# A two-layer conditioned linear-attention block on one core: x and h transposed by DMA instead of TensorE

## The chip, the cores and the metric

The kernel runs on one core of one Trainium2 chip. The metric is the device time in microseconds of one execution. Engines are named TensorE (PE in the rows), VectorE (DVE), ScalarE (ACT), GpSimd (POOL) and SyncE (SP, which here only issues transfers).

## What is computed

x is (8, 512, 512) in float32: 8 batches of 512 tokens with 512 features. Two layers of the same form follow each other, the first with 8 heads, the second with 16:

```python
xn = layernorm(x) * ln_w + ln_b
q, k, v = xn @ Wq + bq, xn @ Wk + bk, xn @ Wv + bv     # masked tokens leave k and v
q = softmax(q by head, over features)
k = softmax(k, over tokens)
att = k^T v by head;  y = q att
scale, shift = split(silu(cond) @ W_emb + b_emb)       # per batch, "film"
h = (layernorm(y) * ln2_w + ln2_b) * (1 + scale) + shift
x = x + silu(h) @ W_out + b_out
```

## The kernel before, in words

A unit is one batch in one layer; there are 16 units, 0 to 7 in layer 0 and 8 to 15 in layer 1. A unit's token array of 512 x 512 is held as four tiles of 128 tokens, or, turned, as four tiles of 128 features. Every matrix product is done in float16 with each float32 operand split in a high and a low part, three products for one: hi x hi, hi x lo, lo x hi (`split_pairs`). So a stage of four tiles has 48 matmuls.

Each engine has its own program, one `step(u, front, back, following)` after the other: front is the unit whose keys, values and queries are made, back is unit u - 1, whose output is finished, following is u + 1, whose x is prepared. The orders are written by hand, and semaphores join them.

- TensorE: K of unit u (features on partitions), YT (16 float32 transposes of unit u - 1's normalised y, L451), V, Q, attention (48 matmuls of 128 columns into `att_ps`), XT (16 transposes of unit u + 1's normalised x, L451), O (the output product of unit u - 1), Y (48 matmuls of 128 columns).
- VectorE: keys masked from PSUM with their maximum (L835), the statistics of x (L798), the gate that finishes h (L881), low halves of the keys (L861), values (L893), queries: bias, maximum and centring (L922, L925, L927) with their low half (L907), sums of q, the residual (L819), y times 1/sum (L956) and its statistics (L960 to L968).
- ACT: y normalised (L1060), exponents of the keys (L1065), their high half (L1073), tanh and the affine of h from PSUM (L1087, L1094), high half of h (L1055), of the values, x normalised (L1038), exponent and high half of q (L1120, L1124), x's affine after the transpose and its high half (L1045, L1050).
- POOL: the power that gives y_rstd (L1166), the output bias added to x (L1185), x_rstd (L1162), low halves of h (L1215), v (L1176), attention (L1180) and x (L1171), the mask of the next unit (L1193, L1201).
- SP: k's high and low half and q's high and low half are transposed by DMA from SBUF to SBUF (`turn`, L331), 128 x 2048 float16 each. Between them go the loads of x, the store of the result and the mask.

Of the kernel before, what the change touches and what calls it, by code (L numbers as in the profile page):

```python
# [29 lines left out]
RMAX = bass.bass_isa.ReduceOp.max  # L41
# [28 lines left out]
def slot(name, i):  # L70

    return 3 if name == "O'" else slot("O", i) if name == "Y" else SLOTS.index((name, i)) % RING


def previous_user(name, i, u):

    place, now = order(u).index((name, i)), u
    while True:
        if place == 0:
            now = now - 1  # L80
            if isinstance(now, int) and now < -1:
                return None
            place = len(order(now))
            continue
        place -= 1
        before, n = order(now)[place]
        if slot(before, n) == slot(name, i):
            return before.rstrip("'"), n, now + OFFSET[before.rstrip("'")] - (before == "O'")


def build(nc, x_d, emb_d, mask0_d, mask1_d, w_d, bias_d, wemb_d, cols_d, ident_d, blocks_d, out_d):
    with ExitStack() as ctx:
# [12 lines left out]
        w_stage = sb("w_stage", [P, C, D], F32)  # L105

        xh_or_h = sb("xh_or_h", [P, T, D], F32)  # L110
# [42 lines left out]
        ones = sb("ones", [P, P], F32)
# [252 lines left out]
        def _(pe):  # L406
# [17 lines left out]
            def nothing(i):  # L424
                pass
# [869 lines left out]
```

## Time and profile before

| | us |
|---|---|
| median of three runs | 895.27 (894.33 to 895.29) |
| the profiled execution | 894.88 |
| its span | 893.1 |
| TensorE busy | 835.5 (94%) |
| VectorE busy | 717.4 (80%) |
| ScalarE busy | 537.0 (60%) |
| GpSimd busy | 382.5 (43%) |
| DMA engines, mean share | 40% |

The span runs from the first to the last instruction on the core. Busy is the time in which an engine had at least one instruction under way; matmuls overlap, and their ends are modelled. The granted clock of TensorE, a share of 2.4 GHz, was 0.98 on the mean.

### The profile page before, as it was taken

The page shows a single profiled execution, that of the slowest core. Times are in us where ns is not written, and L with a number is a line of the kernel's source. Part 1 is how long each engine was busy: PE and PEld are TensorE (multiplying, and loading weights), DVE is VectorE, ACT ScalarE, POOL GpSimd, SP SyncE. Part 2 cuts the span into 40 slices and gives each one's busy share as a digit, 9 for nine tenths or more (in the row PEclk, how much of TensorE's full clock was granted, in tenths as well). Part 3 has the DMA queues.
Part 4 walks back from the last instruction along what each step waited for, and adds up shares of the span by engine and source line. Part 5 has one row for each costly group of instructions (what it writes and reads, how often), then busy time and mean ns, then how long its engine had stood idle before and what let it go on. Part 6 is the DMA issues. An engine that isn't in the chain of part 4 may idle for free.

```text
span 893.1 us, 13959 instructions
## 1 busy us (share of the span) xinstructions
PE 835.5 (94%) x5245; PEld 457.8 (51%) x5245; DVE 717.4 (80%) x1510; ACT 537.0 (60%) x915; POOL 382.5 (43%) x328
## 2 busy tenths in 40 slices
PE   3677999999999999999999999999999999999967
PEld 2225454464555446455555545555454645555444
DVE  5898897898888788887868978687786978687675
ACT  4356384957757595874837467473838567473713
POOL 1053355434545543453554336455534536455402
PEclk9898999999999999999999999999999999999988
DMA  9922335442525434261644325244343324223322
GB/s 322 349 47 48 106 48 108 94 107 50 138 61 143 106 95 108 50 186 61 189 107 95 95 40 110 64 95 107 95 106 81 88 52 110 73 48 95 48 48 94
DMA packets 162419, 90.83 MB, mean 102 GB/s; under 512 B 134672, under 2 KB 134960, under 8 KB 162352
## 3 DMA queue, kind: packets, MB, share of 16 engines
q1 hardware_dynamic: 162352, 89.94, 39.7%
q8 instruction: 41, 0.67, 0.3%
q14 instruction: 26, 0.21, 0.1%
HBM read 39.60 MB, written 16.78 MB: 63 GB/s over the span
## 4 chain that ended last, share of the span: by engine, by line
PE 63%; DVE 14%; ACT 8%; issue 7%; POOL 4%; DMA 3%; SPq 1%; DVEq 0%; POOLq 0%
PE ring L418 53%; PE ring L451 4%; PE att_ps L418 3%; POOL sb_ht_lo L1215 2%; DVE sb_v_or_q L922 2%; DVE sb_q_max L925 2%; ACT sb_k_or_qt L1065 2%; ACT sb_kq_hi L1073 2%; ACT sb_tanh L1087 2%; ACT sb_xh_or_h L1094 1%; POOL sb_v_parts L1176 1%; DVE sb_y_stats L960 1%; DVE sb_kt_or_y L956 1%; DVE sb_w_lo L720 1%; DVE sb_tanh L907 1%
## 5 line engine op out<-in xcount | busy, mean ns | idle before, releaser
L418 PE MATMUL ring<-sb_w_hi,sb_xt_hi 128*128 128x512 f16 x512 | 195.1, 381 | 4.5 <-DVE sb_k_max L835 2.3
L418 PE MATMUL ring<-sb_w_lo,sb_xt_hi 128*128 128x512 f16 x512 | 195.1, 381 | 0.0
L418 PE MATMUL ring<-sb_w_hi,sb_xt_lo 128*128 128x512 f16 x512 | 194.9, 381 | 0.0
L1060 ACT ACTIVATE sb_kt_or_y<-sb_kt_or_y,sb_y_add,sb_y_rstd 128x512 f32<-128x512 f32 x64 | 46.9, 804 | 167.7 <-DVE sb_y_add L968 167.7
L1215 POOL TENSOR_TENSOR sb_ht_lo<-sb_xh_or_h,sb_ht_hi 128x512 f16<-128x512 f32 x60 | 68.4, 1170 | 114.4 <-ACT sb_ht_hi L1055 114.4
L418 PE MATMUL ring<-sb_xt_hi,sb_w_hi 128*128 128x512 f16 x256 | 97.8, 382 | 7.3 <-DVE sb_xt_lo L997 7.3
L418 PE MATMUL ring<-sb_xt_hi,sb_w_lo 128*128 128x512 f16 x256 | 97.8, 382 | 0.0
L418 PE MATMUL ring<-sb_xt_lo,sb_w_hi 128*128 128x512 f16 x256 | 97.8, 382 | 0.0
L418 PE MATMUL ring<-sb_w_hi,sb_ht_hi 128*128 128x512 f16 x240 | 91.0, 379 | 3.9 <-ACT sb_xh_or_h L1045 3.3
L418 PE MATMUL ring<-sb_w_hi,sb_ht_lo 128*128 128x512 f16 x240 | 91.0, 379 | 0.0
L418 PE MATMUL ring<-sb_w_lo,sb_ht_hi 128*128 128x512 f16 x240 | 91.0, 379 | 0.0
L1120 ACT ACTIVATE sb_v_or_q<-sb_v_or_q 128x512 f32<-128x512 f32 x64 | 40.4, 632 | 80.0 <-DVE sb_v_or_q L927 80.0
L418 PEld LDWEIGHTS ring<-sb_w_hi,sb_xt_hi 128*128 128x128 f16 x512 | 50.6, 99 | 65.7 <-issue 4.7
L418 PEld LDWEIGHTS ring<-sb_w_hi,sb_xt_lo 128*128 128x128 f16 x512 | 50.3, 98 | 61.0 <-issue 1.1
L1185 POOL TENSOR_TENSOR sb_x<-sb_x,sb_bias_o 128x512 f32<-128x512 f32 x64 | 80.7, 1290 | 0.0
L1171 POOL TENSOR_TENSOR sb_xt_lo<-sb_xh_or_h,sb_xt_hi 128x512 f16<-128x512 f32 x60 | 67.6, 1158 | 30.6 <-ACT sb_xt_hi L1050 30.6
L418 PEld LDWEIGHTS ring<-sb_w_lo,sb_xt_hi 128*128 128x128 f16 x512 | 50.3, 98 | 58.5 <-issue 1.0
L1176 POOL TENSOR_TENSOR sb_v_parts<-sb_v_or_q,sb_v_parts 128x512 f16<-128x512 f32 x64 | 76.9, 1233 | 7.0 <-ACT sb_v_parts L1106 7.0
L1065 ACT ACTIVATE sb_k_or_qt<-sb_k_or_qt,sb_k_shift 128x512 f32<-128x512 f32 x64 | 45.4, 710 | 47.7 <-DVE sb_k_shift L843 47.7
L1180 POOL TENSOR_TENSOR sb_att_lo<-sb_att,sb_att_hi 128x512 f16<-128x512 f32 x16 | 18.5, 1159 | 120.9 <-ACT sb_att_hi L1126 120.9
L922 DVE SCALAR_TENSOR_TENSOR sb_v_or_q<-ring,sb_scale_down,sb_bias_q 128x512 f32<-128x512 f32 x64 | 47.7, 745 | 22.9 <-POOL sb_v_parts L1176 20.8
L835 DVE CUSTOM_DVE_ANT_0 sb_k_or_qt<-ring,sb_mask_add,sb_scale_down 128x512 f32<-128x512 f32 x64 | 46.5, 745 | 24.2 <-issue 24.2
(186 smaller groups left out, 1757.8 us busy)
## 6 DMA issues: line engine op xcount, KB each, us to landing
out<-sb_x SPq DMA_DIRECT2D x15, 1024.0 KB, 4.9
sb_x<-out SPq DMA_DIRECT2D x8, 1024.0 KB, 5.8
sb_x<-in_x SPq DMA_DIRECT2D x7, 1024.0 KB, 6.3
sb_mask_raw<-in_mask SPq DMA_DIRECT2D x16, 256.0 KB, 5.9
sb_w_stage<-in_L_cond_Wk SPq DMA_DIRECT2D x2, 1024.0 KB, 6.2
sb_w_hi<-in_L_cond_W_emb SPq DMA_DIRECT2D x2, 1024.0 KB, 11.8
sb_w_lo<-in_L_cond_W_emb SPq DMA_DIRECT2D x2, 1024.0 KB, 12.9
sb_wemb<-in_L_cond_film_emb_W SPq DMA_DIRECT2D x2, 1024.0 KB, 6.2
```

Of the source, the lines that this page charges most:

```text
L418: last = nc.tensor.matmul(out, lhs, rhs, start=(n == 0), stop=(n == len(pairs) - 1))
L451: last = nc.tensor.transpose(out[:, j * P:j * P + P], source(i, j), ident[:])
L835: nc.vector.tensor_tensor_reduce(k_or_qt[:, i, :], bank("K", i), mask_add[:], scale_down[:, front, K_:K_ + 1], -3.4e38, ALU.add, ALU.max, ...
L922: nc.vector.scalar_tensor_tensor(out=q[:, t, :], in0=bank("Q", t), scalar=scale_down[:, front, Q_:Q_ + 1], in1=bias_q[front][:], op0=ALU.m ...
L1060: nc.scalar.activation(kt_or_y[:, t, :], kt_or_y[:, t, :], ACT.Identity, bias=y_add[:, t:t + 1], scale=y_rstd[:, t:t + 1]).then_inc(yh_rea ...
L1065: nc.scalar.activation(k_or_qt[:, i, :], k_or_qt[:, i, :], ACT.Exp, bias=k_shift[:, i:i + 1], accum_out=k_sum[:, i:i + 1]).then_inc(k_exp, 1)
L1120: nc.scalar.activation(q[:, t, :], q[:, t, :], ACT.Exp).then_inc(q_exp, 1)
L1171: nc.gpsimd.tensor_tensor(xt_lo[:, c, :], xh_or_h[:, c, :], xt_hi[:, c, :], ALU.subtract).then_inc(xt_lo_ready, 1)
L1176: nc.gpsimd.tensor_tensor(v_lo[:, t, :], v[:, t, :], v_hi[:, t, :], ALU.subtract).then_inc(v_lo_ready, 1)
L1180: nc.gpsimd.tensor_tensor(att_lo[:], att[:], att_hi[:], ALU.subtract).then_inc(att_lo_ready, 1)
L1185: nc.gpsimd.tensor_tensor(xt(unit, t), xt(unit, t), bias_o[layer][:], ALU.add).then_inc(x_biased, 1)
L1215: nc.gpsimd.tensor_tensor(lo[:, c, :], xh_or_h[:, c, :], hi[:, c, :], ALU.subtract).then_inc(ht_lo_ready, 1)
```

## The change

Everything between the products is arranged anew; the products themselves and their number stay.

1. **x by DMA.** ACT normalises x in token order, rounds it to float16 (`tok_hi`), POOL makes the low part (`tok_lo`), and SP transposes both in two halves each (`turn_x`, behind Q of tile 1 and of tile 3). The weight and the bias of the norm are folded into the projection weights (scaled by ln_w per input row) and their biases (a small product of ln_b with the weights, `shift_parts`, `shift_sums`, `fold`). TensorE still turns x of unit 0.
2. **h by DMA.** y stays in token order. VectorE centres it (`centre`: minus the mean, times a row g), applies rstd and a row s (`affine`), ACT takes the tanh, VectorE gates. The rows g and s of each unit come from a table in DRAM (`film_d`), loaded by `load_rows` into all partitions, 512 KB. The high and low part of h are transposed by `turn_h`. TensorE still turns h of the last unit.
3. **Orders.** In VectorE and ACT, h of unit u - 1 and the keys of unit u are interleaved (`keys_beside_h`, `h_beside_keys`). The low half of q goes from VectorE to POOL. On ACT, x of the next unit is normalised before the exponents of q. The statistics of x run two units ahead, behind the sums of q. In units 0 and 15 the queries are made before the values. Low parts of the weights of layer 1 and of W_out are made on POOL.
4. **Start and end.** Five small loads go through ACT's queue. The last unit finishes h tile by tile (`tail`).

The core of the diff; names not shown are as above. Lines of the programs of ACT and VectorE before:

```diff
-        act.wait_ge(y_affine_ready, u)
...
-            nc.scalar.activation(kt_or_y[:, t, :], kt_or_y[:, t, :], ACT.Identity, bias=y_add[:, t:t + 1],
-                                 scale=y_rstd[:, t:t + 1]).then_inc(yh_ready, 1)
...
-        act.wait_ge(k_shift_ready, u + 1)
...
-            nc.scalar.activation(k_or_qt[:, i, :], k_or_qt[:, i, :], ACT.Exp, bias=k_shift[:, i:i + 1],
...
-            turned = nc.scalar.activation(tanh[:, c % 2, :], bank("YT", c), ACT.Tanh, bias=film_now[:, 1, c:c + 1],
...
-            nc.scalar.activation(xh_or_h[:, c, :], bank("YT", c), ACT.Identity, bias=film_now[:, 3, c:c + 1],
-                                 scale=film_now[:, 2, c:c + 1]).then_inc(film_read, 1)
...
-        normalise_x(u + 1, following, u if back is not None else None)
...
-            nc.scalar.activation(q[:, t, :], q[:, t, :], ACT.Exp).then_inc(q_exp, 1)
...
-            nc.scalar.activation(kq_hi[:, t * D:t * D + D], q[:, t, :], ACT.Copy, scale=ONE).then_inc(q_hi_ready, 1)
...
-        nc.scalar.copy(att_hi[:], att[:]).then_inc(att_hi_ready, 1)
...
-        turned_x(u + 1, following)
...
-        def low_q(t):
-            dve.wait_ge(q_hi_ready, 4 * u + t + 1)
-            nc.vector.scalar_tensor_tensor(out=q_lo[:, t * D:t * D + D], in0=q[:, t, :], scalar=ONE,
...
-                low_q(t - 1)
...
-        low_q(T - 1)
```

VectorE now:

```diff
+def centre(unit, t):
+    dve.wait_ge(rows_loaded, 16 * (unit + 1))
+    nc.vector.scalar_tensor_tensor(out=kt_or_y[:, t, :], in0=kt_or_y[:, t, :], scalar=y_mean_var[:, t, 0:1],
+                                   in1=rows_now[:, 0, :], op0=ALU.subtract, op1=ALU.mult).then_inc(y_scaled, 1)
+def affine(unit, t):
+    dve.wait_ge(y_scaled, 4 * unit + t + 1)
+    dve.wait_ge(y_rstd_ready, unit + 1 + (t if unit == LAST else 0))
+    nc.vector.scalar_tensor_tensor(out=kt_or_y[:, t, :], in0=kt_or_y[:, t, :], scalar=y_rstd[:, t:t + 1],
+                                   in1=rows_now[:, 1, :], op0=ALU.mult, op1=ALU.add).then_inc(z_ready, 1)
+def keys_beside_h(u):
+    for t in range(T):
+        centre(u - 1, t)
+    masked_keys(u, 0)
+    affine(u - 1, 0)
+    affine(u - 1, 1)
+    masked_keys(u, 1)
+    gate(u - 1, 0)
+    affine(u - 1, 2)
+    masked_keys(u, 2)
+    gate(u - 1, 1)
+    affine(u - 1, 3)
+    masked_keys(u, 3)
+    key_shift(u)
+    gate(u - 1, 2)
+    gate(u - 1, 3)
+def step(u):
+    keys_beside_h(u)
...
+    values(u, 0)
...
+        x_affine(u + 1)
+    key_sums(u)
+    values(u, 1)
...
+    low_keys(u, 0)
+    low_keys(u, 1)
+    values(u, 2)
+    low_keys(u, 2)
+    low_keys(u, 3)
+    values(u, 3)
...
+        queries(u, t)
+    mask_attention(u)
+    query_sums(u)
...
+        x_statistics(u + 2)
...
+        find_peak(1, PREPARED[1][u - PREP])
...
+        residual(u - 1, t)
+    attended_all(u)
```

ACT, POOL and SP now:

```diff
+def step(u):
+    h_beside_keys(u)
+    high_values(u, (0,))
+    high_keys(u)
+    high_values(u, (1, 2, 3))
...
+        scale_and_split(0, O_)
+        copy_film(1, 0)
...
+    normalise(u + 1, (0, 1))
+    normalise(u + 1, (2, 3))
...
+        high_queries(u, t)
...
+    high_attention(u)
...
+def normalise(unit, tiles):
+    act.wait_ge(x_affine_ready, unit + 1)
+    if unit > 1:
+        act.wait_ge(k_lo_ready, 4 * unit)
+        act.wait_ge(ht_hi_ready, 16 * (unit - 1))
+        act.wait_ge(h_lo_ready, 4 * (unit - 1))
+    for t in tiles:
+        if t >= 2:
+            act.wait_ge(xp_lo_ready, 4 * (unit - 1) + t - 1)
+        nc.scalar.activation(normalised(unit, t), xt(unit, t), ACT.Identity, bias=x_add[:, t:t + 1],
+                             scale=x_rstd[:, t:t + 1]).then_inc(xh_ready, 1)
+    for t in tiles:
+        act.wait_ge(xh_ready, 4 * unit + t + 1)
+        nc.scalar.copy(tok_hi[:, t, :], normalised(unit, t)).then_inc(xp_hi_ready, 1)
...
+    y_power(u - 1)
+    add_bias(u)
+    low_h(u - 1)
+    low_values(u)
...
+    mask_for(u + 1)
+    low_x(u + 1)
+    low_queries(u)
+    low_attention(u)
...
+        x_power(u + 2)
...
+    turn_h(u)
+    turn_k(u)
...
+        load_x(u + 2)
...
+        load_rows(u)
...
+        turn_x(u)
+    turn_q(u)
...
+        sp.wait_ge(x_new, 4 * u)
+        sp.dma_start(out_d[(u - 1) % B].rearrange("(t p) d -> p t d", p=P), xu(u - 1)).then_inc(out_stored, 16)
```

The start: VectorE's order in unit 0, then what TensorE puts between the key tiles and ahead of the values.

```diff
+    find_peak(0, Q_)
+    masked_keys(0, 0)
+    find_scale(0, Q_)
+    split_low(Q_)
...
+    masked_keys(0, 1)
+    find_peak(0, V_)
+    masked_keys(0, 2)
+    find_scale(0, V_)
+    fold(0, K_)
+    masked_keys(0, 3)
+    key_shift(0)
+    split_low(V_)
+    fold(0, Q_)
+    fold(0, V_)
+    queries(0, 0)
+    queries(0, 1)
...
+    queries(0, 2)
+    queries(0, 3)
+    x_statistics(1)
...
+    gather_film(0)
...
+            film_scales(0)
+    y_moments(0, range(T))
+    x_statistics(2)
+    find_peak(0, O_)
...
+    def with_k(i):
+        if i == 0:
+            sum_w(0, Q_)
+            shift_parts(0, V_)
+        elif i == 1:
+            sum_w(0, V_)
+            shift_sums(0, V_)
...
+    project_keys(0, with_k)
...
+    project_tokens("Q", 0, Q_, xt_hi, xt_lo)
...
+    project_tokens("V", 0, V_, xt_hi, xt_lo, between=with_v)
...
+    pe.wait_ge(shift_folded, folded(0, V_))
+    attention(0)
```

The order of instructions shows two places. The first is on VectorE in layer 1, between y of one unit and the keys of the next. `sb_kt_or_y` is y, `ring` the PSUM banks, `sb_spare` a word that makes VectorE wait, `sb_k_or_qt` the masked keys. Before:

```order
L963 BN_AGGR sb_y_mean_var<-sb_y_stats 128x2 x4
L965 TENSOR_SCALAR sb_y_var<-sb_y_mean_var 128x4
L968 SCALAR_TENSOR_TENSOR sb_y_add<-sb_y_mean_var,sb_y_rstd 128x4
L825 COPY sb_film_now<-sb_film 128x16
L663 MEMSET sb_spare 128x1
L835 ISA sb_k_or_qt,sb_k_max<-ring,sb_mask_add,sb_scale_down 128x512
```

Now, in the same place:

```order
L949 TENSOR_SCALAR sb_y_var<-sb_y_mean_var 128x4
L953 SCALAR_TENSOR_TENSOR sb_kt_or_y<-sb_kt_or_y,sb_y_mean_var,sb_rows_now 128x512 x4
L732 MEMSET sb_spare 128x1
L859 ISA sb_k_or_qt,sb_k_max<-ring,sb_mask_add,sb_scale_down 128x512
L859 ISA sb_k_max 128x1
L959 SCALAR_TENSOR_TENSOR sb_kt_or_y<-sb_kt_or_y,sb_y_rstd,sb_rows_now 128x512 x2
L732 MEMSET sb_spare 128x1
L859 ISA sb_k_or_qt,sb_k_max<-ring,sb_mask_add,sb_scale_down 128x512
L859 ISA sb_k_max 128x1
L964 SCALAR_TENSOR_TENSOR sb_kt_or_y<-sb_tanh,sb_kt_or_y 128x512
L959 SCALAR_TENSOR_TENSOR sb_kt_or_y<-sb_kt_or_y,sb_y_rstd,sb_rows_now 128x512
```

Four centrings of y stand ahead of the first key tile now, and affines and a gate (the row that reads `sb_tanh`) between the key tiles. The copy of film and the product that made y_add are gone.

The second place is on ACT in layer 1, from the high half of h (`sb_ht_hi`, seen before) and the values (`sb_v_parts`) to the exponents of q (`sb_v_or_q` onto itself). `sb_kq_hi` is the high half of k or q, `sb_xh_or_h` and, in the change, `sb_k_or_qt` the normalised x, `sb_tok` its float16 parts. Before:

```order
L1055 CAST sb_ht_hi<-sb_xh_or_h 128x512 x4
L1112 CAST sb_v_parts<-sb_v_or_q 128x512 x4
L1038 ACTIVATE sb_xh_or_h<-sb_x,sb_x_add,sb_x_rstd 128x512 x4
L1120 ACTIVATE sb_v_or_q<-sb_v_or_q 128x512
L1124 ACTIVATE sb_kq_hi<-sb_v_or_q 128x512
```

Now:

```order
L1264 CAST sb_v_parts<-sb_v_or_q 128x512
L1237 ACTIVATE sb_kq_hi<-sb_k_or_qt,sb_k_recip 128x512 x4
L1264 CAST sb_v_parts<-sb_v_or_q 128x512 x3
L1221 ACTIVATE sb_k_or_qt<-sb_x,sb_x_add,sb_x_rstd 128x512 x2
L1225 CAST sb_tok<-sb_k_or_qt 128x512 x2
L1221 ACTIVATE sb_k_or_qt<-sb_x,sb_x_add,sb_x_rstd 128x512 x2
L1225 CAST sb_tok<-sb_k_or_qt 128x512 x2
L1268 ACTIVATE sb_v_or_q<-sb_v_or_q,sb_ln_one 128x512
L1273 CAST sb_kq_hi<-sb_v_or_q 128x512
```

The keys' high half moved behind the first cast of the values, and x is normalised in two pairs, each with its casts, ahead of the exponents of q. The second pair writes where the first stood, so it waits for POOL's low parts of it.

## Rows read from the trace of the kernel before

**Rows 1.** The page: busy time, and one POOL group.

```profile
PE 835.5 (94%) x5245; PEld 457.8 (51%) x5245; DVE 717.4 (80%) x1510; ACT 537.0 (60%) x915; POOL 382.5 (43%) x328
...
L1171 POOL TENSOR_TENSOR sb_xt_lo<-sb_xh_or_h,sb_xt_hi 128x512 f16<-128x512 f32 x60 | 67.6, 1158 | 30.6 <-ACT sb_xt_hi L1050 30.6
```

**Rows 2.** Windows: length, busy of PE, PEld, DVE, ACT, POOL, clock, DMA.

```profile
570.49:621.46 50.97, 50.45 (x322) 27.63 (x320) 39.99 (x83) 31.04 (x55) 24.00 (x21) 1.00 0.37 89
```

**Rows 3.** TensorE's timeline: start us, us, engine line op [idle before].

```profile
594.97 2.84 PE L418 MATMUL att_ps<-sb_kt_or_y,sb_v_parts 128*128 128x128 f16 x48
597.65 1.92 PE L451 MATMUL ring<-sb_ident,sb_xh_or_h 128*128 128x128 f32 x16
599.41 0.38 PE L418 MATMUL ring<-sb_w_hi,sb_ht_hi 128*128 128x512 f16 x1
...
610.45 0.22 PE L418 MATMUL ring<-sb_att_hi,sb_k_or_qt 128*128 128x128 f16 x1 [0.52 <-issue]
```

**Rows 4.** The same timeline, SP's queue.

```profile
604.66 2.30 SPq L335 DMA_TRANSPOSE sb_k_or_qt<-sb_tanh  x1
```

**Rows 5.** L335 on SP: issue ns min/median/max, first and last start.

```profile
L335 SPq DMA_TRANSPOSE sb_k_or_qt<-sb_kq_hi x16: 1317/1810/1987, 78.9 to 854.8; - x16
...
DMA to landing us min/median/max: 4.3/4.7/7.6
```

**Rows 6.** POOL's timeline: the power behind y's variance, units 0, 10, 14.

```profile
93.53 1.03 POOL L1166 TENSOR_TENSOR sb_y_rstd<-sb_y_var,sb_minus_half 128x4 f32<-128x4 f32 x1 [6.36 <-DVE sb_y_var L965]
...
616.95 1.04 POOL L1166 TENSOR_TENSOR sb_y_rstd<-sb_y_var,sb_minus_half 128x4 f32<-128x4 f32 x1 [6.02 <-DVE sb_y_var L965]
...
818.15 1.04 POOL L1166 TENSOR_TENSOR sb_y_rstd<-sb_y_var,sb_minus_half 128x4 f32<-128x4 f32 x1 [5.35 <-DVE sb_y_var L965]
```

**Rows 7.** Timeline in unit 0, bias additions beside low keys.

```profile
48.18 1.28 POOL L1185 TENSOR_TENSOR sb_x<-sb_x,sb_bias_o 128x512 f32<-128x512 f32 x1
...
49.42 1.71 POOL L1185 TENSOR_TENSOR sb_x<-sb_x,sb_bias_o 128x512 f32<-128x512 f32 x1
...
50.11 1.57 DVE L861 SCALAR_TENSOR_TENSOR sb_k_or_qt<-sb_k_or_qt,sb_k_recip,sb_kq_hi 128x512 f16<-128x512 f32 x1
...
51.09 1.71 POOL L1185 TENSOR_TENSOR sb_x<-sb_x,sb_bias_o 128x512 f32<-128x512 f32 x1
```

**Rows 8.** VectorE lines over the span: ns min/median/max.

```profile
L861 DVE SCALAR_TENSOR_TENSOR sb_k_or_qt<-sb_k_or_qt,sb_k_recip,sb_kq_hi x64: 744/752/1700, 48.3 to 835.0; 128x512 f16<-128x512 f32 x64
...
L881 DVE SCALAR_TENSOR_TENSOR sb_xh_or_h<-sb_tanh,sb_xh_or_h x64: 681/691/1678, 110.3 to 882.7; 128x512 f32<-128x512 f32 x64
...
L922 DVE SCALAR_TENSOR_TENSOR sb_v_or_q<-ring,sb_scale_down,sb_bias_q x64: 736/745/752, 65.7 to 851.1; 128x512 f32<-128x512 f32 x64
```

**Rows 9.** Timeline: POOL's mask operation beside a low half of q.

```profile
594.71 1.93 POOL L1201 TENSOR_SCALAR sb_mask_add<-sb_mask_raw 128x512 f32<-128x512 int32 x1
...
595.79 0.68 DVE L907 SCALAR_TENSOR_TENSOR sb_tanh<-sb_v_or_q,sb_kq_hi 128x512 f16<-128x512 f32 x1
```

**Rows 10.** Timeline, 611 to 637: y, exponents, casts of h, values.

```profile
611.39 1.29 DVE L956 TENSOR_TENSOR sb_kt_or_y<-ring,sb_q_recip 128x512 f32<-128x512 f32 x2 [0.67 <-PE ring L418]
...
624.88 0.72 ACT L1065 ACTIVATE sb_k_or_qt<-sb_k_or_qt,sb_k_shift 128x512 f32<-128x512 f32 x1 [2.67 <-DVE sb_k_shift L843]
...
635.46 2.19 ACT L1055 CAST sb_ht_hi<-sb_xh_or_h 128x512 f16<-128x512 f32 x4
...
636.23 2.72 DVE L893 SCALAR_TENSOR_TENSOR sb_v_or_q<-ring,sb_scale_down,sb_bias_v 128x512 f32<-128x512 f32 x4
```

**Rows 11.** TensorE's timeline: the first product of unit 0.

```profile
27.86 0.61 PE L418 MATMUL ring<-sb_xt_hi,sb_w_hi 128*128 128x512 f16 x1 [7.35 <-DVE sb_xt_lo L997]
```

**Rows 12.** Windows in unit 0, columns as in rows 2.

```profile
55.00:60.00 5.00, 2.89 (x14) 1.18 (x13) 4.86 (x14) 0.44 (x1) 0.00 (x0) 1.00 0.56 105
60.00:64.00 4.00, 0.50 (x3) 0.00 (x1) 3.93 (x7) 4.00 (x8) 2.52 (x3) 0.82 0.00 0
64.00:70.00 6.00, 5.93 (x17) 2.49 (x18) 3.88 (x11) 4.85 (x8) 4.14 (x4) 0.55 0.00 1
```

More of the change, by code:

```diff
@@ L70, in slot @@
[L70 to L88, printed above, removed]
+K_, V_, Q_, O_ = range(4)
@@ new lines, with bank_of, previous_user @@
+BANKS = {"K": (0, 1, 2, 3), "first": (4, 5, 0, 1), "second": (2, 3, 4, 5), "O": (0, 1, 2, 3), "Y": (4, 5, 2, 3), "last": (0, 1, 4, 5)}
+def bank_of(name, i, unit):
+    if name in "VQ":
+        name = "first" if (name == "V") != (unit in Q_FIRST) else "second"
+    elif name == "O" and unit == LAST:
+        name = "last"
+    return BANKS[name][i]
+PLACES = [place for u in range(UNITS + 1) for place in order(u)]
+def previous_user(place):
+    here = PLACES.index(place)
+    for before in reversed(PLACES[:here]):
+        if bank_of(*before) == bank_of(*place):
+            return before
+    return None
@@ L460, in film_product, with output @@
[L460 to L468 removed]
+            def output(unit, tiles=range(T)):
+                project_tokens("O", unit, O_, ht_hi, ht_lo, tiles)
@@ L497, in sum_ln @@
-            def sum_ln():
-                pe.wait_ge(ln_peak, LAYERS)
-                for layer in range(LAYERS):
-                    last = nc.tensor.matmul(sums[0][:, 8 + layer:9 + layer], ones[:], peak[:, layer, LN:LN + 1], start=True, stop=True)
-                last.then_inc(ln_summed, 1)
+                last.then_inc(film_turned, 1)
             def bound_film(layer):
                 pe.wait_ge(film_peak, layer + 1)
-                nc.tensor.matmul(sums[1][:, FILM:FILM + 1], ones[:], peak[:, layer, FILM:FILM + 1], start=True, stop=True
-                                 ).then_inc(film_bounded, 1)
@@ L522, in attend @@
+            def attend(u, between=lambda t: None):
                 pe.wait_ge(qt_hi_ready, 16 * (u + 1))
@@ new lines, in last_unit @@
+            def last_unit(u):
+                keys_beside_h(u)
+                queries(u, 0)
+                key_sums(u)
+                queries(u, 1)
+                low_keys(u, 0)
+                low_keys(u, 1)
+                queries(u, 2)
+                low_keys(u, 2)
+                low_keys(u, 3)
+                queries(u, 3)
+                for t in range(T):
+                    values(u, t)
+                residual(u - 1, 0)
+                mask_attention(u)
+                query_sums(u)
+                residual(u - 1, 1)
```

1562 lines of the change are left out of this document (848 added, 714 removed).

## The prediction

> **What bounds the kernel now.** I read the page first, then the stage windows, then one unit of layer 1 in order of time. The page says 835.5 us of TensorE in a span of 893.1, 94% [rows 1]. A unit in the middle tells where that comes from: in 50.97 us TensorE has 50.45 us of work at a granted clock of 1.00, and VectorE is next with 39.99 [rows 2]. In the piece of TensorE's timeline the starts give the prices: attention 2.68 us (594.97 to 597.65), XT 1.76, the four output tiles 10.4 (599.41 to 609.93, less the 0.16 by which a matmul's modelled end runs past the next one's start), then a hole of 0.52 and Y [rows 3]. YT costs what XT does, K, V and Q what O does, and Y about what attention does: 4 x 10.4 + 2 x 2.68 + 2 x 1.76 = 50.5 us. The program is bound by TensorE. The hole is small, but the reader should look at what ends it: q's low half is issued for transposing at 604.66 [rows 4] and a transpose lands 4.7 us after its issue in the median [rows 5], at 609.4, just before the output tiles end. So the chain queries, exponent, split, transpose is nearly as long as its cover.
>
> As marks I take the start of the power on POOL that turns y's variance into y_rstd: 93.53 for unit 0, 818.15 for unit 14, 51.76 us a unit [rows 6]. Thus 93.5 us of start, 724.6 for 14 units, 75.0 of tail. The profiled execution took 894.88 us, 1.8 more than its span and 0.4 under the median of the three runs shown.
>
> **What the change does to each engine in a unit.**
> TensorE loses 32 transposes, 3.5 us, and needs 46.9 us. If it stayed the bound, the 14 units would give back about 49 us.
> ACT loses 12 tile operations: normalising y, the affine of x, and the affine of h. It had 31 us in a unit and is no bound.
> VectorE gains the centring and the affine of y, 8 tile operations. It gives q's low half to POOL, 4. Net 4 x 0.7 = 2.8 us on 40 [rows 2], still under 46.9.
> POOL gains q's low half, 4 subtractions at 1.16 [rows 1], on 24.0 us.
> SP issues 10 transposes instead of 4. Four of the ten are half as large, so it is the work of eight: at 1.8 us for a high half and 2.3 for a low one [rows 4, 5], SP goes from 8 us to 16, plus one load of 512 KB. That is room enough, but SP takes them in order: q waits behind x.
> By busy time the change wins. The loop from one y to the next decides otherwise.
>
> **VectorE against POOL.** In unit 0, the only place where they met, low keys (two operands in SBUF) ran at 1.57 us beside POOL's bias additions, and POOL's additions rose from 1.28 to 1.71 us; the pairs are 1.67 us apart [rows 7]. The same VectorE operation takes 0.75 in the median (1.70 at most), and in the last unit the gate took 1.68 at most against 0.69 [rows 8]. So an operation with two SBUF operands waits for the POOL addition in front of it, and the next addition for it. Operations that read PSUM do not: the bias of q has 752 ns at most [rows 8]. The Trainium skill (SBUF — State Buffer, "SBUF: two separate sides") says that the port pair is an exclusive lock held for the whole instruction, against any GpSimd operation that reads SBUF. By that rule the one-input mask operation would hold VectorE too; here a low part of q beside it kept its 0.68 us [rows 9], so I charge additions and subtractions only. Neither reading changes the sum, since what meets the mask is off the loop.
> The old order keeps the two apart (POOL adds the bias while VectorE reads keys from PSUM). The new one puts four centrings and two affines beside the same additions, and gates and low keys beside POOL's subtractions.
>
> **The loop of one unit in layer 1**, from y's variance (0). A VectorE tile operation follows the last by 0.67 us, an ACT cast by 0.55, an exponent by 0.72 [rows 10].
> 1. Two centrings, 1.34; two more and two affines each in a pair with an addition, 4 x 1.67 = 6.7: 8.0. The first key tile hides in there.
> 2. Seven more (keys, gates, affines) 4.7; one gate behind a subtraction 0.45; the key shift with its waits 0.75: 13.9. Before, keys went first, 7.8 us after the variance: exponents began at 624.88 against 616.95 [rows 6, 10].
> 3. ACT: four exponents at 0.72 with two casts of h between, and the handover: 4.2, 18.1.
> 4. Key sums 0.4. Three value tiles at 0.67 and four low keys at 0.86, 5.45, with one to two waits behind POOL, 0.8 to 1.8: 24.7 to 25.7.
> 5. The last value: cast 0.65; POOL subtraction 1.15, mask 1.95, and two subtractions of x 2.3. ACT can normalise x's last tile only then (two buffers): 0.75 and two casts 1.1. Together 7.9, 32.6 to 33.6.
> 6. ACT's four exponents and casts of q wait behind these in its queue: 4 x 1.33, 37.9 to 38.9.
> 7. SP: high half 1.85, low half landed 4.8 after: 44.6 to 45.6.
> 8. Y's first tile and handover 0.8, then four products, four statistics and moments 5.5 (611.39 to 616.9 [rows 10]): **51.0 to 52.0, taken as 51.5**.
> TensorE's 46.9 us fit inside, so it waits about 4.7 us a unit, some before attention (low keys land at 29 at the earliest) and some before Y.
>
> Layer 0 adds the mask to each value tile and a copy on POOL: 1.5, 53. Units 3 to 6 also have a weight peak (2.3 us and 0.5) between x's statistics and the residual; it leaves 1.8 on the loop, 54.8. Unit 1 has the split of the output weight on ACT before x: eight operations and a copy, 6 us, 59. Low weights now on POOL, folds and the scales stand beside waits and cost nothing; if the loop fell to TensorE's 46.9, they would cost up to 1 us each.
> Sum of 14: 59 + 2 x 53 + 4 x 54.8 + 7 x 51.5 = 744.7, against 724.6: **+20.1**.
>
> **Start.** The first K matmul is at 27.86 [rows 11]. The bound of ln is gone and x needs no affine, so it can start near 21. But then TensorE stands: the key tiles wait for V's peak (VectorE, behind Q's peak and split), the queries for a fold behind V's split. I reach attention 1 us later than before, and then VectorE has the film products, x's statistics for two units and a weight peak (3.1 and 2.8 us) before the first centring, at 101. Bounds: 93 (TensorE's early start kept) and 108. Taken **+7.5**.
>
> **Tail.** Queries first takes q's transpose (4.7 to land) out of the last unit's path; the values come last. By the same prices their low parts are ready 36.7 after the variance of unit 14; attention 2.7, mask, two splits and Y's first tile 3.4: 42.8. Then h is finished tile by tile: 23 VectorE tile operations at 0.67 and four sets of moments at 0.6 to the last gate, 60.6; transpose, cast and low part 2.2, 12 matmuls 2.6, residual 0.8, store 2.3: 68.5 against 75.0, **-6.5** (bounds -12 and +2).
>
> Sum: 894.9 + 20.1 + 7.5 - 6.5 = **916 us**, 2.3% slower.
>
> **Rivals.**
> A, faster. The pairs in steps 1, 2 and 4 do not form, or the loop overlaps more than I let it. Without any lock the loop is 51.5 - 4.0 - 0.45 - 0.8 = 46.2 and TensorE bounds: 47 in layer 1, 49 to 51 in layer 0, with start and tail as above 850; with half of it 882. It decides at 1.5 us a unit: under 50.0 in layer 1 the kernel is faster. For it: all busy times [rows 2]; ACT and SP have room. Against it: the pairs in rows 7. Chance 0.33.
> B, much slower: the clock. TensorE's granted clock fell towards half (1.2 GHz of 2.4) after a hole of 3.5 us at 60 and not after one of 2.1 at 55: the windows show 2.9 us of TensorE in 5 at 1.00, then 0.5 in 4, then 0.55 of the clock [rows 12]. My hole before Y is 2.7 us. If it drops each unit, Y itself doubles, +2.7 on the loop, x14 = 38: 954. Chance 0.12.
> C, level: loop and start errors cancel within 0.2%. Chance 0.04.
> The forecast has the rest, 0.51, with 895 to 940 as its own range.
>
> **The numbers.** About 0.2% is what a measurement of this kernel can tell from no change. Faster is A, 0.33; same C, 0.04; slower the rest, 0.63. The range 862 to 948 leaves out A's best end and B's worst: loop 47.6 to 54, start and tail at their bounds.
>
> **What would show it.** Right: POOL's powers 51 to 52 us apart in layer 1; centrings and the first affines at 1.6 us beside the bias additions; TensorE idle about 2 us before attention and 2 to 3 before Y, ended by the q transpose; exponents of q queued behind x's casts. Wrong: powers under 50 us apart, TensorE without holes, centrings at 0.75; or a granted clock of half in the middle of the program.

## The result

The changed kernel takes 982.65 us, median of four runs (980.25 to 983.43), against 894.8 for the kernel before (893.96 to 895.29): a ratio of 1.098, 95% interval 1.096 to 1.100. The direction was right; the forecast of 916 and its range, which ended at 948, were not. One execution of the kernel with the fourteen extra products below took 1021.9 us at a mean granted clock of 0.83, which was at 0.81 already in the 590 us before the first of these products, and is left out where times are compared.

The page of the changed kernel, its busy line, TensorE's clock in 40 slices and the start of the chain that ended last:

```profile
PE 834.8 (85%) x4865; PEld 433.7 (44%) x4865; DVE 813.9 (83%) x1521; ACT 437.1 (45%) x757; POOL 522.9 (53%) x411
...
PEclk9887987999799797999897999999999999899989
...
DVE 28%; PE 21%; ACT 20%; issue 15%; POOL 11%; DMA 5%; SPq 0%; DVEq 0%; ACTq 0%; POOLq 0%
```

TensorE issues 380 instructions fewer than in [rows 1] and is busy for the same 835 us: it ran the rest at a lower clock (0.93 on the mean against 0.98). In the chain it now has 21% of the span, where it had 63%, and VectorE, ScalarE and POOL have 59% together: a loop through all engines sets the time. One unit of layer 1, from one power of y to the next (columns as in [rows 2]):

```profile
641.92:694.60 52.68, 47.88 (x286) 25.23 (x284) 47.95 (x85) 23.44 (x41) 31.69 (x25) 0.97 0.64 136
```

Against [rows 2] TensorE is 2.6 us shorter, VectorE 8 longer where I had counted 2.8: the rest is waiting for POOL, which the profile shows as long instructions (low keys, affines, centrings and gates of y, the centring of q: 0.68 to 0.75 us each where nothing is in the way, up to 1.75 here). With the power of y as mark, as in [rows 6], the span splits so:

| us | before | forecast | changed | missed by |
|---|---|---|---|---|
| start, to the power of unit 0 | 93.5 | 101 | 110.8 | 9.8 |
| unit 1 | 56.1 | 59 | 70.1 | 11.1 |
| unit 2 | 51.3 | 53 | 54.8 | 1.8 |
| units 3 to 5 | 155.7 | 164.4 | 186.6 | 22.2 |
| units 6 and 7 | 104.6 | 107.8 | 113.5 | 5.7 |
| units 8 to 14 | 357.0 | 360.5 | 371.4 | 10.9 |
| tail, to the end of the span | 75.0 | 68.5 | 73.9 | 5.4 |

So 43 of the 67 us that were missed lie in the start, in unit 1 and in units 3 to 5, and 11 in the seven units that the loop was worked out for. Four things in the trace bear on this. First the pairs of VectorE and POOL, in the timeline of the unit above:

```profile
641.75 0.75 DVE L953 SCALAR_TENSOR_TENSOR sb_kt_or_y<-sb_kt_or_y,sb_y_mean_var,sb_rows_now 128x512 f32<-128x512 f32 x1
641.92 1.44 POOL L1400 TENSOR_TENSOR sb_y_rstd<-sb_y_var,sb_minus_half 128x4 f32<-128x4 f32 x1 [9.80 <-DVE sb_y_var L949]
...
643.34 1.60 POOL L1406 TENSOR_TENSOR sb_x<-sb_x,sb_bias_o 128x512 f32<-128x512 f32 x1
643.74 1.75 DVE L953 SCALAR_TENSOR_TENSOR sb_kt_or_y<-sb_kt_or_y,sb_y_mean_var,sb_rows_now 128x512 f32<-128x512 f32 x1
644.90 1.72 POOL L1406 TENSOR_TENSOR sb_x<-sb_x,sb_bias_o 128x512 f32<-128x512 f32 x1
...
646.09 2.75 DVE L959 SCALAR_TENSOR_TENSOR sb_kt_or_y<-sb_kt_or_y,sb_y_rstd,sb_rows_now 128x512 f32<-128x512 f32 x2
```

The centring that meets an addition takes 1.75 us (1.67 forecast), and two affines take 2.75 (3.3). Only one centring of the four is caught: the power comes first on POOL, and the additions begin at 643.34, when two centrings are done and the third is under way. Next, SP's queue and the hole before Y in the same unit:

```profile
669.84 9.77 SPq L340 DMA_TRANSPOSE sb_xt_parts<-sb_tok  x4
680.55 1.93 SPq L340 DMA_TRANSPOSE sb_k_or_qt<-sb_kq_hi  x1
682.60 2.41 SPq L340 DMA_TRANSPOSE sb_k_or_qt<-sb_tanh  x1
...
687.37 0.22 PE L471 MATMUL ring<-sb_att_hi,sb_k_or_qt 128*128 128x128 f16 x1 [3.73 <-issue]
```

q's low part is issued 40.7 us after the power and Y starts 4.8 later, at 45.4. TensorE has stood 3.7 us by then, and that has a price, seen in the windows over the next unit's hole (737 to 740), the first part of Y and the rest:

```profile
737.00:740.00 3.00, 0.00 (x0) 0.00 (x0) 2.88 (x7) 0.00 (x0) 1.03 (x1) 0.87 0.92 175
...
740.00:742.60 2.60, 2.56 (x25) 2.60 (x26) 0.69 (x1) 0.00 (x0) 0.00 (x0) 0.50 0.68 249
742.60:747.50 4.90, 4.90 (x43) 3.01 (x41) 4.64 (x12) 0.00 (x0) 0.00 (x0) 0.99 0.48 139
```

The clock is 0.50 (1.2 GHz) for the first 2.6 us of Y. In each of the units 8 to 14 TensorE stands 3.2 to 4.2 us before Y, and Y's products then take 4.1 to 5.3 us, against 2.8 in the kernel before. Last, the waits that end in TensorE's order, over the whole span (who waited for whom: us, times, longest):

```profile
PE att_ps L558 <- ACT sb_rows_now L1195: 19.3, 2, 9.7
PE film_ps L508 <- ACT sb_rows_now L1201: 8.6, 2, 6.5
PE att_ps L556 <- ACT sb_rows_now L1195: 8.6, 1, 8.6
...
PE film_ps L518 <- ACT sb_rows_now L1201: 7.4, 1, 7.4
```

L556 and L558 are the sums of the bias shift of layer 1's weights, in units 3, 4 and 5, between V and Q on TensorE. L508 and L518 are the second half of layer 1's film product and its transposes, both in unit 1. All wait for a small copy that stands in ScalarE's queue behind the values, or behind the exponents of q.

### The profile page after: what moved, and what is told of

Same layout as the page of the kernel before. It is cut to its first block, busy times and chain, and to the rows that moved or that the text cites. A ratio compares the mean times of both kernels' runs of the same rounds, so it can differ in the third digit from the quotient of the medians.

```text
span 981.1 us, 13639 instructions
## 1 busy us (share of the span) xinstructions
PE 834.8 (85%) x4865; PEld 433.7 (44%) x4865; DVE 813.9 (83%) x1521; ACT 437.1 (45%) x757; POOL 522.9 (53%) x411
## 4 chain that ended last, share of the span: by engine, by line
DVE 28%; PE 21%; ACT 20%; issue 15%; POOL 11%; DMA 5%; SPq 0%; DVEq 0%; ACTq 0%; POOLq 0%
PE ring L471 17%; POOL sb_v_parts L1417 5%; ACT sb_k_or_qt L1229 4%; DVE sb_kt_or_y L959 4%; DMA sb_k_or_qt<-sb_kq_hi 4%; ACT sb_kq_hi L1237 3%; DVE sb_kt_or_y L953 3%; POOL sb_tok L1425 3%; ACT sb_v_or_q L1268 3%; DVE sb_y_stats L941 3%; ACT sb_kq_hi L1273 3%; DVE sb_kt_or_y L936 3%; DVE sb_kt_or_y L964 2%; PE att_ps L471 2%; DVE sb_x_stats L844 2%
## 5 line engine op out<-in xcount | busy, mean ns | idle before, releaser
L471 PE MATMUL ring<-sb_w_hi,sb_xt_parts 128*128 128x512 f16 x1024 | 313.4, 385 | 4.8 <-DVE sb_bias_q L780 4.8
L471 PE MATMUL ring<-sb_w_lo,sb_xt_parts 128*128 128x512 f16 x512 | 196.9, 385 | 0.0
L1247 ACT ACTIVATE sb_tanh<-sb_kt_or_y,sb_scale_down 128x512 f32<-128x512 f32 x64 | 46.2, 722 | 313.7 <-DVE sb_kt_or_y L959 312.3
L471 PE MATMUL ring<-sb_w_hi,sb_ht_parts 128*128 128x512 f16 x512 | 158.1, 384 | 4.5 <-DVE sb_kt_or_y L936 3.5
L471 PEld LDWEIGHTS ring<-sb_w_hi,sb_xt_parts 128*128 128x128 f16 x1024 | 101.6, 99 | 134.0 <-issue 10.9
L471 PE MATMUL ring<-sb_xt_parts,sb_w_hi 128*128 128x512 f16 x512 | 156.1, 387 | 1.1 <-issue 1.1
L1417 POOL TENSOR_TENSOR sb_v_parts<-sb_v_or_q,sb_v_parts 128x512 f16<-128x512 f32 x56 | 74.0, 1330 | 68.7 <-ACT sb_v_parts L1264 68.5
L1412 POOL TENSOR_TENSOR sb_tok<-sb_kt_or_y,sb_tok 128x512 f16<-128x512 f32 x60 | 70.1, 1168 | 68.3 <-ACT sb_tok L1254 67.4
L471 PE MATMUL ring<-sb_w_lo,sb_ht_parts 128*128 128x512 f16 x256 | 98.5, 385 | 0.0
L471 PE MATMUL ring<-sb_xt_parts,sb_w_lo 128*128 128x512 f16 x256 | 98.3, 384 | 0.0
L1430 POOL TENSOR_TENSOR sb_tanh<-sb_v_or_q,sb_kq_hi 128x512 f16<-128x512 f32 x64 | 75.9, 1208 | 23.2 <-ACT sb_kq_hi L1273 22.9
L1425 POOL TENSOR_TENSOR sb_tok<-sb_k_or_qt,sb_tok 128x512 f16<-128x512 f32 x56 | 69.3, 1257 | 20.7 <-ACT sb_tok L1225 20.1
L471 PEld LDWEIGHTS ring<-sb_xt_parts,sb_w_hi 128*128 128x128 f16 x512 | 50.4, 100 | 62.1 <-issue 7.7
```

Source lines behind the costliest of these rows:

```text
L471: last = nc.tensor.matmul(out, lhs, rhs, start=(n == 0), stop=(n == len(pairs) - 1))
L1247: nc.scalar.activation(tanh[:, t % 2, :], kt_or_y[:, t, :], ACT.Tanh, scale=scale_down[:, layer, FILM:FILM + 1]).then_inc(tanh_ready, 1)
L1412: nc.gpsimd.tensor_tensor(tok_lo[:, t, :], kt_or_y[:, t, :], tok_hi[:, t, :], ALU.subtract).then_inc(h_lo_ready, 1)
L1417: nc.gpsimd.tensor_tensor(v_lo[:, t, :], v_of(u)[:, t, :], v_hi[:, t, :], ALU.subtract).then_inc(v_lo_ready, 1)
L1425: nc.gpsimd.tensor_tensor(tok_lo[:, t, :], source, tok_hi[:, t, :], ALU.subtract).then_inc(xp_lo_ready, 1)
L1430: nc.gpsimd.tensor_tensor(q_lo[:, t * D:t * D + D], q[:, t, :], kq_hi[:, t * D:t * D + D], ALU.subtract).then_inc(q_lo_ready, 1)
```

## The experiments

Eight kernels ran, one of them twice. Each time is the median of its runs; the kernel before, run beside them on the same chips, took 896.1 to 896.4.

**The copy of the shift first.** ScalarE's step:

```diff
     h_beside_keys(u)
+    if PREP <= u < PREP + 3:
+        copy_shift(1, PREPARED[1][u - PREP])
     high_values(u, (0,))
...
-    elif PREP <= u < PREP + 3:
-        copy_shift(1, PREPARED[1][u - PREP])
```

> Units 3 to 5 of the changed kernel take 61.6 to 63.2 us from one power of y to the next, where the neighbours 6 and 7 take 56.7, and TensorE stands 8.6 to 9.7 us behind the values, at the sum of the bias shift, until ScalarE has copied the shift (L1195), which stands behind all values in its queue. Here that copy is issued right behind the exponents of the keys; nothing else moves. Theory W (a wait put in TensorE's order): TensorE stands under 1 us there, the three units fall to about 56.7, together 16 to 18 us, 965 us in all. Theory L (the loop through the queries and DMA sets these units as well, and the hole is only where its slack shows): the copy adds 0.6 us to the loop, the hole moves ahead of Y, and the time stays within 4 us of 982.6.

Measured: 963.1 us (ratio to before 1.074, 1.072 to 1.076), 19.6 less than the change. Units 3 to 5 take 167.7 us instead of 186.6, and no idle time is left in front of L558. Theory W holds and L falls. The wait alone was worth 19 of the 22 us by which these units were missed.

**The bias additions late.** POOL's step (the last unit likewise):

```diff
     y_power(u - 1)
-    add_bias(u)
     low_h(u - 1)
...
     low_attention(u)
+    add_bias(u)
```

> POOL's four bias additions move from beside the centrings, affines and key tiles to behind the low part of the attention, where VectorE reads PSUM or one SBUF operand. Theory P (the pairs of two-operand instructions, as priced in the forecast): centrings and first affines go from 1.67 us apart to 0.67, the loop of a unit falls by 2.5 to 4 us where nothing else takes over, 15 units, so 940 to 955 us; bias additions at 1.25 us instead of 1.66. Theory K (the keys' products on TensorE set the pace of that stretch, the pairs only fill it): the end of the gates stays at 14.7 us after y's variance and the time stays within 8 us of 982.6.

Measured: 933.2 us (1.042, 1.039 to 1.045), 49.4 less, the largest of the single edits and 7 us beyond what theory P asked for. VectorE's timeline right behind y's variance, in unit 10, and all bias additions of the span (ns min/median/max):

```profile
609.19 2.73 DVE L953 SCALAR_TENSOR_TENSOR sb_kt_or_y<-sb_kt_or_y,sb_y_mean_var,sb_rows_now 128x512 f32<-128x512 f32 x4
...
612.52 1.41 DVE L959 SCALAR_TENSOR_TENSOR sb_kt_or_y<-sb_kt_or_y,sb_y_rstd,sb_rows_now 128x512 f32<-128x512 f32 x2
```

```profile
L1406 POOL TENSOR_TENSOR sb_x<-sb_x,sb_bias_o x64: 1251/1270/1760, 21.1 to 902.7; 128x512 f32<-128x512 f32 x64
```

Four centrings take 2.73 us instead of 3.74, two affines 1.41 instead of 2.75, an addition 1.27 instead of 1.72 in the median. The gates end 2.8 us earlier, so theory P's mechanism holds and K falls. A unit of layer 1 falls by 3.5 us, from 53.1 to 49.6. The other 0.7 fits the clock: in units 8, 10, 12 and 14 the hole before Y is 1.2 to 1.7 us and the granted clock of Y stays at 1.00, and in units 9, 11 and 13, after holes of 2.2 to 2.7 us, it still falls (0.62 over Y). But the unit does not fall to 46.2, as the forecast had it for a loop without pairs.

**Products nobody reads in the hole.** TensorE, units 8 to 14, ahead of Y:

```diff
+    if u >= B:
+        for _ in range(14):
+            nc.tensor.matmul(film_ps[:], w_hi1[:, 0, 0, 0:P], w_hi1[:, 0, 0, :], start=True, stop=True)
     attend(u)
```

> In units 8 to 14 fourteen products of 512 columns that nobody reads, about 3.0 us, go into an idle PSUM bank between the output tiles and Y, where TensorE stands 3.2 to 4.2 us. The work of the reference is all there. Theory C (the clock): the granted clock in the first 2.6 us of Y goes from 0.5 to 1.0, Y's chain to the variance falls from 7.5 to about 6.3 us, each of the seven units by 1.2, 8 us in all, 974. Theory D (Y is slow because the store of the result, the mask and the transposes run beside it): the clock stays up but the time does not move, or TensorE ends later by what the products overlap, +0 to +5 us.

Measured: 973.9 to 976.7 us (1.088, 1.086 to 1.090). The same kernel once more:

> The fourteen products nobody reads once more, the whole work of the reference beside them, for a trace that can be compared: the profiled execution of the first time had a mean granted clock of 0.83 and 1021.9 us, the three others 973.9 to 976.7. Theory C (clock): in the profile the clock of Y in units 8 to 14 is 1.0, the holes before Y are gone, the unit takes 52.0 us instead of 53.2, 974 to 976 us. Theory R (the extra products themselves bring the clock down for long stretches in some executions): one or more executions come over 1000 us again with a mean clock near 0.83.

Measured: 974.1 us (1.088, 1.085 to 1.090), 8.5 less than the change, with more work in it. All four executions lie between 973.0 and 976.0, and the low clock of the one at 1021.9 was there before its first extra product, so nothing here speaks for theory R. A window over the last product nobody reads, Y and the next keys shows the clock of theory C:

```profile
684.00:691.00 7.00, 6.34 (x65) 4.18 (x64) 5.97 (x12) 0.00 (x0) 0.00 (x0) 1.00 0.66 202
```

Units 8 to 14 take 52.2 us on the mean instead of 53.1, and from Y to the power they take 6.5 in all seven, instead of 7.0 to 7.9. Theory C holds and D falls. So the clock costs 0.9 us a unit here, somewhat less than the 1.2 that was expected, and 6.3 us in all: the other 2 of the 8.5 lie in the start and the tail, which the edit does not touch, so that the total met the expected 974 in part by luck.

**q before x in layer 1.** ScalarE, with POOL (where the mask goes last) and SP in the same order, and four tiles of their own for the normalised x:

```diff
     normalise(u + 1, (0, 1))
-    normalise(u + 1, (2, 3))
+    if u < B:
+        normalise(u + 1, (2, 3))
     for t in range(T):
         high_queries(u, t)
     high_attention(u)
+    if u >= B:
+        normalise(u + 1, (2, 3))
```

> In units 8 to 14 the normalised x of the next unit gets its own four tiles (the stage buffer of layer 1's weights, free by then), so ScalarE normalises tiles 0 and 1, then makes the exponents of q, then the attention's high part, then tiles 2 and 3; POOL and SP follow that order, and the mask of the next unit goes last on POOL. Theory Q (the queue order of step 5 of the forecast holds q back): the exponents of q end with the queries, at about 36.5 us after the variance instead of 38.8, Y begins at 43 instead of 45.5, each of the seven units falls by 2 to 2.5 us and, if the hole before Y falls under 2 us and the clock stays up, by another 1.2: 14 to 25 us, 958 to 968. Theory X (x becomes the late one): its second half lands at 49 to 52 us, TensorE stands before the keys instead of before Y, and the gain is under 5 us.

Measured: 959.8 us (1.072, 1.070 to 1.074), 22.8 less: units 8 to 14 at 50.1 instead of 53.1. SP's queue in unit 10 of that kernel:

```profile
662.19 5.58 SPq L340 DMA_TRANSPOSE sb_xt_parts<-sb_tok  x2
670.35 1.77 SPq L340 DMA_TRANSPOSE sb_k_or_qt<-sb_kq_hi  x1
672.23 2.25 SPq L340 DMA_TRANSPOSE sb_k_or_qt<-sb_tanh  x1
674.59 3.30 SPq L340 DMA_TRANSPOSE sb_xt_parts<-sb_tok  x2
```

The power before it is at 634.27, so q's low part goes out at 38.0 instead of 40.7, and x's second half has left SP by 43.6 and lands at 45.5, just before TensorE begins the next keys at 45.6. Theory Q holds and X falls: the order of step 5, the mask in it, held q back by 2.7 us. The hole before Y is 0.8 to 1.7 us and Y's clock 1.00 in all seven units. From Y to the power most still take 7.2 us and not 6.5, since VectorE, behind x's statistics and the residual, gets to Y's first tile 1.6 us after Y began (678.84 against 677.20).

**The three together.** The edits one, two and four.

> The three edits together: copy of the shift right behind the key exponents, bias additions late, q before x in units 8 to 14. Alone they took 19.6, 49.4 and 22.8 us off 982.6. Theory S (the three lie on one loop and add, less the clock, which the late bias had already kept up in units 8 to 14): units 8 to 14 go from 49.7 to 47.3, units 3 to 5 from 59 to 53, and 896 to 901 us in all. Theory B (VectorE becomes the bound: it is busy 46.8 of 50 us with the bias late): units 8 to 14 stay at 48.5 or more and the time is 905 or more.

Measured: 903.9 us (1.009, 1.007 to 1.011). Units 8 to 14 fall to 47.5 us, little more than the 46.9 that the forecast gave TensorE, as theory S had it; units 3 to 5 come to 53.8. Theory B falls. The total missed S's range by 3 us. (The late bias alone had kept the clock up in four of these seven units, not in all of them.)

**q first from unit 2 on.** As above, with x of units 3 to 8 in the unused quarter of layer 1's weights, and on TensorE:

```diff
+    attend(u)
     if PREP <= u < PREP + 4:
         sum_w(1, PREPARED[1][u - PREP])
-    attend(u)
```

> As before, and q before x from unit 2 on (x of units 3 to 8 gets four tiles in the still unused space of layer 1's W_out), and the sum of a weight's peak goes behind Y on TensorE instead of ahead of it. Theory S: each of units 2 to 7 falls by 2 to 2.5 us as units 8 to 14 did, and units 3 to 6, where TensorE waits 5 to 6 us ahead of Y for the peak that VectorE finds, by 1 to 3 more: 16 to 26 us less than with the three edits. Theory F (the peak itself, 2.8 us between x's statistics and the residual on VectorE, sets those units): units 3 to 6 keep 2 to 3 us more than units 2 and 7, and 12 to 16 us less in all.

Measured: 886.9 us (0.990, 0.988 to 0.993), 17 less, and below the kernel before. Unit 2 fell by 2.5, units 3 to 6 by 2.2 each and unit 7 by 3.7, which is 15 us. Nothing more came from the sum behind Y, and units 3 to 5 stay 3 us above unit 2, which speaks for theory F (VectorE's search for the peak lies on the loop). Unit 6 has such a search too and takes no more than unit 7, 50.4 us, and the total lies in S's range and 1 us outside F's, so this is not settled.

**The start and unit 1.** VectorE's first unit, and ScalarE in unit 1:

```diff
     find_scale(0, Q_)
+    find_peak(0, V_)
     split_low(Q_)
...
     x_affine(1)
+    find_peak(0, O_)
+    find_scale(0, O_)
+    x_statistics(2)
...
-    x_statistics(2)
-    find_peak(0, O_)
...
+    if u == 1:
+        copy_film(1, 1)
     for t in range(T):
         high_queries(u, t)
-    if u == 1:
-        copy_film(1, 1)
```

The split of W_out (`scale_and_split(0, O_)` and its low part) moves with the sum of its peak from unit 1 into unit 0, `fold(0, Q_)` ahead of the last key tile, and TensorE's `bound_film(1)` behind Y.

> As before, and the start and unit 1 rearranged: V's peak ahead of Q's low part, Q's fold ahead of the last key tile, W_out's peak, scale and split and the statistics of unit 2 into the stretch of unit 0 in which VectorE and ScalarE idle (78 to 92 us), the copies of the film product of layer 1 ahead of the exponents of q, its bound behind Y. Theory G (the extra 11 us of unit 1 and 5 to 9 us of the start are waits in the queue of ScalarE and VectorE that TensorE stands for): the first power of y comes at 97 to 101 us instead of 108, unit 1 takes 52 to 56 us instead of 66, together 17 to 24 us less. Theory H (the copies and products of the film, 7 us of TensorE and 6 us of ScalarE in unit 1, cost what they last wherever they stand): unit 1 stays over 60 us.

Measured: 860.7 us (0.962, 0.959 to 0.965). The first power comes at 93.6 us instead of 111.4, unit 1 takes 58.6 instead of 66.6, 26 us in all, more than theory G asked for in the start and less in unit 1. Theory H falls, though narrowly. These edits were not run one by one. The page's busy line and one unit of layer 1 of this kernel:

```profile
PE 798.3 (93%) x4865; PEld 410.9 (48%) x4865; DVE 772.1 (90%) x1521; ACT 436.4 (51%) x757; POOL 505.5 (59%) x411
```

```profile
598.66:646.03 47.37, 45.63 (x283) 23.40 (x282) 45.06 (x85) 23.48 (x41) 30.66 (x25) 1.00 0.69 151
```

TensorE is the bound again, at 47.4 us a unit against 51 in [rows 2], with VectorE, at 45.1, close behind. The transposes by DMA do give back the 3.5 us that the forecast counted, once nothing else stands in the way.

**The mask beside the centrings.** POOL, on top of the last kernel:

```diff
     y_power(u - 1)
+    if u > 1:
+        mask_for(u)
...
     low_x(u + 1, (2, 3))
-    mask_for(u + 1)
```

> The kernel of the last run (860.7 us) with POOL's mask operation (one input tensor from SBUF, 1.93 us) moved from behind the low parts of x to right behind the power of y, where VectorE runs the four centrings (two inputs from SBUF, 0.746 us each, 0.69 apart). Theory O (only POOL instructions with two inputs take turns with VectorE's; one with one input slows them a little, as 0.69 to 0.81 us for the centring of q beside the mask in the changed kernel): centrings 0.75 to 0.9 us, the gates end 0 to 0.5 us later, time within 5 us of 860.7. Theory A (any POOL instruction that reads SBUF holds VectorE's two-input instructions for its whole length): one centring takes 1.9 us or more in each unit, the gates end 1.5 to 2 us later, and with TensorE's slack in the unit used up the time rises by 10 to 25 us.

Measured: 889.4 us (0.992, 0.989 to 0.995), 28.7 more. VectorE and POOL behind y's variance in unit 11 of that kernel:

```profile
619.61 3.08 DVE L968 SCALAR_TENSOR_TENSOR sb_kt_or_y<-sb_kt_or_y,sb_y_mean_var,sb_rows_now 128x512 f32<-128x512 f32 x4
623.51 0.75 DVE L874 CUSTOM_DVE_ANT_0 sb_k_or_qt<-ring,sb_mask_add,sb_scale_down 128x512 f32<-128x512 f32 x1 [0.82 <-issue]
```

```profile
621.31 2.16 POOL L1407 TENSOR_SCALAR sb_mask_add<-sb_mask_raw 128x512 f32<-128x512 int32 x1
```

In layer 1 the instructions say O: three centrings keep 0.75 us, the fourth, which begins inside the mask's 2.16 us, takes 1.10 and ends before the mask does. In layer 0 they do not. There the mask, which also reads a scale per partition, takes 2.91 us instead of 2.00 and the centrings keep 0.75:

```profile
203.89 2.91 POOL L1402 TENSOR_SCALAR sb_mask_add<-sb_mask_raw,sb_mask_scale 128x512 f32<-128x512 f32 x1
```

That looks as if the mask had waited for the centrings, which end at 205.01. The Trainium skill (SBUF — State Buffer, "SBUF: two separate sides") has a GpSimd operation that reads SBUF and a VectorE operation with two SBUF inputs exclude each other for the whole instruction. The bias additions of this kernel behave so beside the centrings (0.75 us becomes 1.75), the mask of layer 0 may, and the mask of layer 1 does not; what makes the two masks differ no run shows.

The time lies above both theories, for a reason that neither had: the mask of this unit's own keys now comes behind the power, so the first key tile waits for it (0.82 us idle here, 1.8 in layer 0). Units 8 to 14 take 48.6 instead of 47.3, 9 of the 28.7 us, and 17 lie in units 2 to 7. The loop is the bound again.

## Why the prediction was wrong

**What bounds the kernel, and the loop.** Right. TensorE lost its place to the loop from one y to the next. Step by step in unit 10, counted from the power at 641.92, forecast first: second affine 8.0, trace 6.9; key shift 13.9 and 13.2; exponents of the keys 18.1 and 17.1; x's last cast 32.6 to 33.6 and 33.3; last cast of q 37.9 to 38.9 and 38.5; q landed 44.6 to 45.6 and 45.4. Up to the exponents the loop was 0.7 to 1.1 us ahead of its forecast, and from x's casts on it was inside. So two errors cancel: the pairs were priced at 4.45 us up to the gates and cost 2.8 (run with the bias late), and the stretch from the exponents to x's casts was about 1 us longer than its sum.

**Step 8, Y.** Here the loop failed: 6.3 us forecast (6.5 from Y to the power in [rows 3, 6]), 7.2 and 7.7 in units 10 and 11. "My hole before Y is 2.7 us. If it drops each unit" was put off as rival B with a chance of 0.12. The hole was 3.2 to 4.2 us and the clock fell to half in all seven units, in six of them for a part of Y and in unit 13 for all of it: 0.9 us a unit (the extra products), not 2.7. That is some 6 of the 10.9 us in units 8 to 14; of the rest, q landed at 45.5 on the mean against the 45.1 taken, and 6.3 was 0.2 short of the 6.5 at full clock. Units 6 and 7 (5.7 us missed) show the same: 7.9 and 9.8 us from Y to the power, in unit 7 after a hole of 5.0.

**"Low weights now on POOL, folds and the scales stand beside waits and cost nothing."** The step that failed worst. It took them as work to be hidden, and the work is small: 0.6 us of ScalarE, 2 of TensorE. But each is a wait in the order of TensorE, on something that stands late in ScalarE's queue. In units 3 to 5 TensorE stood 8.6 to 9.7 us between V and Q, Q came late, and the loop behind it. 22 us, of which the first run shows 19.

**Unit 1, 59 us.** The same error. The split of W_out and the first film copy were counted as 6 us of ScalarE; that TensorE waits for this copy, and for the second one behind the exponents of q, was not, and it stood 6.5 and 7.4 us for them. In the kernel with the rearranged start the split is out of the unit and the second copy stands ahead of the exponents. Both holes are gone and the unit is 8 us shorter than in the kernel before it, at 58.6; how much of the 8 is the copies' and how much the split's, no run shows.

**The start, +7.5 against +17.3.** The bound of 108 was passed as well (the kernels that leave the start alone reach the first power at 107.9 to 111.8). What I had right was VectorE's work behind y's statistics of unit 0 (x's statistics and the peak of W_out, 106.6 to 112.1 in the trace). It shows in the mark too, since POOL makes x's power first, and that one waits for x's statistics. The step that failed is "I reach attention 1 us later than before". Attention of unit 0 began at 87.4 us, against 74.7 in the kernel before: TensorE stood 5.9 us for V's peak and 4.8 for Q's fold, and then 6.6 for the last low part of v:

```profile
87.40 0.91 PE L471 MATMUL att_ps<-sb_v_parts,sb_kt_or_y 128*128 128x128 f16 x7 [6.61 <-POOL sb_v_parts L1417]
```

In the queues of ScalarE and POOL the values came behind all four queries. So attention was 11.7 us behind its forecast, of which 1.9 were got back by the mark. The rearranged start reaches the power at 93.6, so 17 to 18 us of it were order, not work; which of its moves gave what was not taken apart.

**The tail, -6.5 us against -1.1.** The low parts of v were ready at 36.2 us behind the power (36.7 forecast). Then TensorE started attention after a hole of 5.9 us, at a clock of 0.60:

```profile
943.60:948.40 4.80, 4.78 (x50) 4.68 (x51) 0.09 (x1) 0.00 (x0) 0.00 (x0) 0.60 0.11 21
```

4.8 us where 2.7 were counted. Behind the last gate TensorE's transposes, casts, low parts and products follow each other tile by tile, 10.9 us where 7.9 were counted. No run took the tail alone.

**Rivals.** A gave the loop 46.2 us without pairs. The run with the bias late has 49.6: without the pairs of the additions, the queue order of step 5 (2.7 us) still held q, and in three units of seven the clock still fell. It took both edits to reach 47.5. B was the right mechanism at a third of its price. C did not happen. The chances of the sign were fair; the range was too narrow: its upper end took a longer loop and the bounds of start and tail, and nothing for a wait that the extra steps of units 1 and 3 to 5 could bring. Nor is 948 the sum of its terms: a loop of 54 in all 14 units (+35), a start at 108 (+7) and a tail at +2 (+8.5) give 966 us, still short of 982.65.

## What to carry to other kernels

Price a small helper step by what its engine's queue holds in front of its input, not by its length: an in-order TensorE that waits for a 0.6 us copy at the end of ScalarE's values stands for all of them. When work leaves the bounding engine, first list what else closes the loop, queue by queue (here: POOL additions beside VectorE, x in front of q on ScalarE, POOL and SP), since the change pays only once the last of these is out of the way: 982.7 us as given, 860.7 with the same transposes, the queues reordered and four tiles of its own for x, against 896.4 before. And holes of 3.2 to 4.2 us before Y cost Y half its clock for most of its products here, 0.9 us a unit, which a few products nobody reads gave back.

## What was not expected of the hardware

Fourteen extra products a unit made the kernel 8.5 us faster (974.1 against 982.65), 6.3 of it in the units that have them, by keeping the granted clock at 1.00 through Y.

POOL's power on 128 x 4 elements takes 1.03 us in [rows 6] and 1.44 in the changed kernel, beside a centring: even a tiny instruction with two inputs seems to wait its turn. In unit 0, where a reduction with one input runs beside it, it takes 1.01. No run took this alone.
